# The token stage starts with the first pair of images while the second is relaid, its norm's sums come from the added rows, and tokens are normalised in place

## The reference

```
x2 = input of layer 2 (kept)        # residual of the scans
y  = scans(norm(x2)) + x2           # "rows", NCHW
n  = group_norm(y)                  # 48 channels in 16 groups, per image
t  = n.reshape(b, h*w, 48)          # the same bytes, read as tokens of 48
h  = gelu(gelu(t @ W1 + b1))        # 16 hidden, 8 + 8
u  = x1 * gate(layernorm(x2half))   # depthwise 3x3 + pointwise + product
out = y + u @ W2 + b2
```

## Time and profile before

| what | before |
|---|---|
| median of 3 runs | 2882.09 us |
| the profiled execution | 2881.06 us, span 2879.3 us |
| PE busy | 2431.3 us, 84% |
| DVE busy | 1431.1 us, 50% |
| ACT busy | 835.9 us, 29% |
| POOL busy | 250.1 us, 9% |
| end of the last scan | about 2424.4 us |
| first instruction of `affine(0)` | 2597.9 us |
| reduction of line 1324 in `mlp(0)`, (1), (2), (3) | 2636.1, 2702.3, 2764.7, 2828.9 us |

### The profile page before, as it was taken

One profiled execution on the slowest core, in us unless ns is written; L12 is line 12 of the kernel. 1 busy time (PEld: TensorE's weight loads), 2 busy tenths in 40 slices (PEclk: granted clock), 3 DMA queues, 4 the chain that ended last, 5 costly groups with the idle time before them and its releaser, 6 DMA issues.

```text
span 2879.3 us, 47164 instructions
## 1 busy us (share of the span) xinstructions
PE 2431.3 (84%) x18580; PEld 2126.0 (74%) x18580; DVE 1431.1 (50%) x3238; ACT 835.9 (29%) x1347; POOL 250.1 (9%) x244
## 2 busy tenths in 40 slices
PE   2999999999998899999999608999999996006876
PEld 2999939849832899999999608999999996002433
DVE  3323263353365444445555664444455555785565
ACT  3433353353456002430035320024300353002221
POOL 1000000000000720000000130000000001453110
PEclk9999999999999999999999859999999998557988
DMA  8840000012003200000000292000000001573333
GB/s 153 144 72 4 1 1 1 1 31 58 1 1 86 47 1 1 1 1 1 1 1 1 39 267 46 1 1 1 1 1 1 1 1 44 176 262 88 88 88 88
DMA packets 52147, 129.90 MB, mean 45 GB/s; under 512 B 9728, under 2 KB 34656, under 8 KB 45504
## 3 DMA queue, kind: packets, MB, share of 16 engines
q1 hardware_dynamic: 48864, 113.92, 16.6%
q10 hardware_dynamic: 2976, 13.34, 1.5%
q0 software_dynamic: 128, 0.01, 0.0%
HBM read 76.91 MB, written 50.33 MB: 44 GB/s over the span
## 4 chain that ended last, share of the span: by engine, by line
PE 78%; DVE 7%; DMA 6%; ACT 4%; issue 3%; POOL 1%; SPq 0%; ACTq 0%; DVEq 0%; POOLq 0%
PE bank L938 17%; PE bank L939 15%; PE bank L940 15%; PE bank L841 13%; PE bank L903 5%; PE bank L856 3%; PE bank L846 3%; ACT work L616 3%; DMA flat_rows<-work 2%; PE bank L975 2%; DVE work L319 2%; DMA work<-saved 2%; PE bank L1033 1%; DMA work<-in_x 1%; PE bank L966 1%
## 5 line engine op out<-in xcount | busy, mean ns | idle before, releaser
L1242 DVE TENSOR_TENSOR image<-bank,image 112x128 f32<-112x128 f32 x2032 | 666.7, 328 | 710.3 <-PE bank L940 710.3
L938 PE MATMUL bank<-image,scan_wt 112*112 112x128 f32 x4064 | 810.9, 280 | 36.8 <-ACT image L690 30.2
L939 PE MATMUL bank<-image,scan_wt 112*112 112x126 f32 x4064 | 770.7, 271 | 0.0
L940 PE MATMUL bank<-image,scan_wt 112*112 112x126 f32 x4064 | 769.4, 270 | 0.0
L938 PEld LDWEIGHTS bank<-image,scan_wt 112*112 112x112 f32 x4064 | 566.6, 175 | 44.2 <-ACT image L690 30.3
L939 PEld LDWEIGHTS bank<-image,scan_wt 112*112 112x112 f32 x4064 | 581.0, 176 | 0.0
L940 PEld LDWEIGHTS bank<-image,scan_wt 112*112 112x112 f32 x4064 | 578.4, 176 | 0.0
L841 PE MATMUL bank<-work 112*128 112x192 f32 x2304 | 423.4, 332 | 10.5 <-issue 10.5
L616 ACT ACTIVATE work<-image,gn_shift,gn_scale 48x567 f32<-48x567 f32 (+5 forms) x384 | 334.8, 904 | 314.3 <-PE bank L846 220.3
L708 ACT COPY work<-image 48x256 f32 (+1 forms) x256 | 109.5, 428 | 978.1 <-PE bank L940 977.6
L841 PEld LDWEIGHTS bank<-work 112*128 112x128 f32 x2304 | 374.5, 192 | 12.9 <-issue 12.4
(11 more groups left out here) (142 smaller groups left out, 1651.6 us busy)
## 6 DMA issues: line engine op xcount, KB each, us to landing
work<-saved SPq DMA_DIRECT2D x64, 384.0 KB, 8.6
flat_rows<-work ACTq DMA_DIRECT2D x32, 384.0 KB, 7.5
image<-flat_rows SPq DMA_DIRECT2D x4, 3072.0 KB, 14.5
out<-image SPq DMA_DIRECT2D x8, 1536.0 KB, 8.1
saved<-image SPq DMA_DIRECT2D x12, 768.0 KB, 10.0
saved<-image SPq DMA_DIRECT2D x6, 1536.0 KB, 16.4
band<-in_x SPq DMA_DIRECT2D x16, 384.0 KB, 5.7
work<-in_x SPq DMA_DIRECT2D x16, 384.0 KB, 5.6
```

The costliest lines, as they stand in the source:

```text
L938: mm(dst, wt[:, 1], src, start=True, stop=False)
L939: mm(dst[:, 1:J2, :], wt[:, 0], src[:, 0:J2 - 1, :], start=False, stop=False)
L940: mm(dst[:, 0:J2 - 1, :], wt[:, 2], src[:, 1:J2, :], start=False, stop=True).then_inc(s_prod[g], 1)
L1242: v.tensor_tensor(line(g, along_w, at), prod, line(g, along_w, src), ALU.add).then_inc(s_state[g], 1)
```

## The change

- The fourth scan of the last layer goes without `exchange`: the result stays split by row parity, and the relayout takes it from there.
- The relayout adds on DVE alone, two instructions of 112 x 1024 for a block (`relayout(t)`, 16 blocks). The sum goes into a part of `image` that is free by then (the first block into `nat`), so no block waits for an earlier one to be sent. `x2` comes into five buffers `kept`; the first five blocks are brought during the last scans.
- A block is sent in four DMAs of 192 KB with runs of 512 bytes in `flat` (`send_rows`): for the first pair the `LO` half by SP and the `HI` half by ACT, for the second pair all four by SP.
- The statistics come from the added rows in SBUF (`rows_stats`, four `bn_stats` of 112 x 512 for a block), not from the loaded tokens, and the group norm runs for each pair; a matrix `group_tok` spreads the sums to the token layout.
- Tokens of images 0 and 1 are loaded when the first pair is sent, and `affine` works in place in `toks`. DVE relays the first pair, takes its statistics, relays two blocks of the second pair, does `affine(0)`, then the other six blocks, three blocks' statistics, `affine(1)`, and the last five blocks' statistics inside `mlp(0)`. Images 2 and 3 get their norm behind `mlp(0)`.
- `residual(b)` waits until PE has turned all tokens of image b (before: until `affine(b)`), as it overwrites them. POOL adds b2 in eight instructions of 768 columns.
- ACT alone takes the turned tokens of image 0, and waits for the last relayout before its gelu. POOL builds its constants for the MLP during the last scans.

```diff
+        def send_rows(queue, t, parity):
+            g, n = t // NBLK, t % NBLK
+            for i in range(2):
+                queue.dma_start(lines[parity, 2 * g + i, :, n * BLK:(n + 1) * BLK, :],
+                                rows_home(t)[(LO, HI)[parity], i, :].rearrange("p (k w) -> p k w", k=BLK))\
+                    .then_inc(s_flat[g][i] if n else s_first[g], 16)
...
+            def bring_kept(t):
+                g, n = t // NBLK, t % NBLK
+                for parity, rows in enumerate((LO, HI)):
+                    sp.dma_start(kept[t % KEPT][rows, :].rearrange("p (w n) -> p w n", w=2),
+                                 halves[:, :, g, parity, n * 2 * BN:(n + 1) * 2 * BN]).then_inc(s_x2[t % KEPT], 16)
+
+            def bring_tokens(b):
+                sp.wait_ge(s_stat, X_STATS + 2 * NB + 1 + b // 2)
+                sp.wait_ge(s_first[b // 2], 64)
+                sp.wait_ge(s_flat[b // 2][b % 2], 32 * (NBLK - 1))
                 sp.dma_start(toks[:, b, :], flat[b].rearrange("(p n) -> p n", p=128)).then_inc(s_tok[b], 16)
+
+            for t in range(KEPT):
+                bring_kept(t)
+            for t in range(NBLK):
+                sp.wait_ge(s_res, t + 1)
+                send_rows(sp, t, 0)
+                if t + KEPT < NBLK:
+                    bring_kept(t + KEPT)
+            for t in range(NBLK, NBLK + KEPT):
+                bring_kept(t)
+                if t == NBLK + 2:
+                    bring_tokens(0)
+            for t in range(NBLK, 2 * NBLK):
+                sp.wait_ge(s_res, t + 1)
+                send_rows(sp, t, 0)
+                send_rows(sp, t, 1)
+                if t + KEPT < 2 * NBLK:
+                    bring_kept(t + KEPT)
+                if t == NBLK:
+                    bring_tokens(1)
+            bring_tokens(2)
+            bring_tokens(3)
...
             def residual(b):
-                sp.wait_ge(s_xn, b + 1)
+                sp.wait_ge(s_xt_p, (b + 1) * GROUPS)
...
+                    for c in range(0, C, SLICE):
+                        last = nc.gpsimd.tensor_tensor(v[:, c:c + SLICE, :], ...
+                    last.then_inc(s_b2, 1)
...
+                if layer == 1:
+                    break
...
+            act.wait_ge(s_res, 2 * NBLK)
             gelu_twice(0)
+            act.wait_ge(s_first[1], 64)
+            act.wait_ge(s_xn, 2)
+            mlp(0, True)
...
+            mlp(0, True)
+            pe.wait_ge(s_add, 2 * NQ + TWO)
+            token_sums(7, 2, NB)
...
+            def relayout(t):
+                g, n = t // NBLK, t % NBLK
+                dve.wait_ge(s_x2[t % KEPT], 32 * (t // KEPT + 1))
+                if t:
+                    dve.wait_ge(s_res, t)
...
+                for i in range(2):
+                    last = v.tensor_tensor(o[:, i], state[:, i], x2[:, i], ALU.add)
+                last.then_inc(s_res, 1)
...
+            relayout(NBLK)
+            relayout(NBLK + 1)
+            dve.wait_ge(s_tok[0], 16)
             affine(0)
+            for t in range(NBLK + 2, 2 * NBLK):
+                relayout(t)
+            for t in range(3):
+                rows_stats(NBLK + t)
+            dve.wait_ge(s_tok[1], 16)
+            affine(1)
...
+            mlp(0, True, False, rows_stats)
+            dve.wait_ge(s_stat, X_STATS + 2 * NB + 2)
+            group_norm(7, P, NSTAT, 2, NB)
+            for b in range(2, NB):
+                dve.wait_ge(s_tok[b], 16)
+            affine(2)
```

More of the change, by code:

```diff
@@ L181, in build @@
         at += 16 * C
[L182 to L190 removed]
+        assert at <= WORK - IN_COLS, at
+        nat = cut(0, [CHUNK], P)
+        at = WORK - KEPT * CHUNK
+        kept = [cut(at + i * CHUNK, [CHUNK], P) for i in range(KEPT)]
+        back = kept[0:PER]
+        swap_tmp = cut(at - 256, [2, 64, 2], P)
+        toks = image[:, :].rearrange("p (b n) -> p b n", b=NB)[:, :, 0:TCOLS]
+        hid = image[:, TCOLS:IMG]
         x_t = [cut(i * 512, [512]) for i in range(2)]
[L192 removed]
+        n_pad = cut(1024, [G, GW])
+        at = 1024 + G * GW
         w1_sb = cut(at, [2 * HID], 97)
@@ L206, in build @@
         at += 5 * 128
-        assert at <= 13300, at
+        assert at <= WORK, at
         gdw_sb = gates[:, 0:72]
@@ L490, in _ @@
                 pool.wait_ge(s_state[g], 1)
-            for m in range(PER):
-                nc.gpsimd.memset(back[m][32:HALF, :], 0.0).then_inc(s_back_gap, 1)
-            pool.wait_ge(s_back_gap, PER)
+            for m in range(KEPT):
+                nc.gpsimd.memset(kept[m][32:HALF, :], 0.0).then_inc(s_back_gap, 1)
+            pool.wait_ge(s_back_gap, KEPT)
             pool.wait_ge(s_const, 16 * N_CONST)
@@ L1039, in _ @@
             pe.wait_ge(s_band, N_BAND + G + 1)
-            with pe.Fori(0, NB - 1) as b:
-                mlp(b, True)
-            mlp(NB - 1, False)
+            mlp(0, True)
+            pe.wait_ge(s_add, 2 * NQ + TWO)
+            token_sums(7, 2, NB)
+            for b in range(1, NB):
+                mlp(b, b + 1 < NB)
         @block.vector
@@ new lines, in rows_stats @@
+            def rows_stats(t):
+                g, n = t // NBLK, t % NBLK
+                dve.wait_ge(s_res, t + 1)
+                for i in range(2):
+                    for h in range(2):
+                        last = take_stats(P, 2 * g + i, 2 * n + h, rows_home(t)[:, i, h * BN:(h + 1) * BN])
+                if n == NBLK - 1:
+                    last.then_inc(s_stat, 1)
+            for t in range(NBLK):
+                relayout(t)
+            for t in range(NBLK):
+                rows_stats(t)
@@ L1340, in row_norm, with mlp @@
                                     ALU.add).then_inc(s_ln, 1)
-            def mlp(b, more, even_more):
+            def mlp(b, more, even_more, behind=None):
                 for i in range(4):
                     row_norm(b, i)
+                    if behind and i < 2:
+                        behind(NBLK + 3 + i)
                     if more:
@@ L1349, in mlp @@
                     take_tokens(b + 1, g)
+                for t in range(5, NBLK if behind else 0):
+                    behind(NBLK + t)
                 dve.wait_ge(s_gt_p, 8 * b + 6)
@@ L1381, in mlp @@
                                         ALU.add).then_inc(s_add, 1)
+            relayout(NBLK)
+            relayout(NBLK + 1)
+            dve.wait_ge(s_tok[0], 16)
             affine(0)
+            for t in range(NBLK + 2, 2 * NBLK):
+                relayout(t)
+            for t in range(3):
+                rows_stats(NBLK + t)
+            dve.wait_ge(s_tok[1], 16)
+            affine(1)
+            dve.wait_ge(s_xn, 2)
             dve.wait_ge(s_gate_zero, 2)
             dve.wait_ge(s_gate_w, 16 * N_GATE)
-            for g in range(1, GROUPS, 2):
-                take_tokens(0, g)
-            affine(1)
-            with dve.Fori(0, NB - 2) as b:
-                chain.enter(b, MLP_LINKS)
-                mlp(b, True, True)
-                chain.leave(NB - 2)
-            mlp(NB - 2, True, False)
-            mlp(NB - 1, False, False)
+            dve.wait_ge(s_first[1], 64)
+            mlp(0, True, False, rows_stats)
[4 more added lines that the diff above has]
+            affine(2)
+            for b in range(1, NB):
+                mlp(b, b + 1 < NB, b + 2 < NB)
 def kernel(**inputs):
```

180 lines of the change are left out of this document (77 added, 103 removed).

## The result

The changed kernel takes 2784.28 us (median of four runs, 2780.75 to 2788.44) against 2879.49 us for the kernel before beside it: a ratio of 0.9677, with a 95% interval of 0.9645 to 0.9709. The forecast was 2780. The execution that was profiled is the slowest of the four, 2788.44 us with a span of 2786.6.

What follows compares the result with a forecast made beforehand. The end stage was taken as latency behind latency, no engine or queue near its limit. -3.8 - 119.0 + 7.3 + 24.9 - 7.8 - 5.3 + 2.5 = -101.2 from 2881.06 gives 2780 us, own range 2764 to 2794.

Steps and rivals of the forecast that it cites:

- Scans (a): Fourth scan of the last layer, without the exchange beside it: 3.8 us less, bounds 0 to 5.
- To `affine(0)` (b): From the last scan step to the start of `affine(0)`: 54.5 us instead of 173.5, a gain of 119.0.
- To the first reduction (c): From `affine(0)` to the reduction of `mlp(0)`: 45.5 us instead of 38.2, a loss of 7.3.
- To the second reduction (d): Reduction of `mlp(0)` to that of `mlp(1)`: 91.0 us instead of 66.15, a loss of 24.9, with image 0's residual late.
- The rest: Later stretches, through holds by POOL's add: `mlp(1)` gains 7.8 us, `mlp(2)` gains 5.3, `mlp(3)` loses 2.5.
- One transfer at a time: Rival: stores and loads of blocks do not overlap in SP's queue; 2805 us, chance 0.20.
- The residual is not late: Rival: image 0's residual comes early enough, so reduction to reduction takes 66 us; 2755 us in all, chance 0.08.
- The 512-byte sends: Rival: slow sends make the kernel slower than before; at 50 GB/s 121 us more, 2901 us, chance 0.03.
- DVE's relayout was held: Rival: the relayout is held at every block, 5 us for each of eight, 40 in all; 2820 us, chance 0.07.

Runs made afterwards that it cites:

- e9: The changed kernel with all sends of the first pair held until its eight blocks are added: 2788.95 us.
- e2: The changed kernel with the load of a block ahead of the sends in SP's queue, and the tokens of image 1 later: 2772.52 us.
- e1: The changed kernel with the residual of image 0 issued ahead of the tokens of images 2 and 3: 2763.84 us.
- e5: The changed kernel with POOL adding b2 in one piece instead of eight: 2783.00 us.
- e4: The changed kernel with sends in runs of 4 KB instead of 512 bytes, so the output is not the reference's: 2777.62 us.
- e7: The changed kernel with e1 and e2 together, plus the second pair's upper halves sent from GpSimd's queue: 2755.72 us.

## Why the prediction was right, step by step

**Scans (a): right.** 3.8 us were forecast, 3.9 measured (685.5 less 681.6). The rate is that of the earlier trace rows without the exchange. The changed kernel, the stretch that had 230 adds before, columns as the earlier trace rows:

```profile
2260.00:2420.00 160.00, 160.00 (x1408) 159.57 (x1408) 82.92 (x235) 0.00 (x0) 0.00 (x0) 1.00 0.00 1
```

In the profiled execution it does not show in the time, since the layer began 3.9 us later there.

**To `affine(0)` (b): the order of events right, 4 us too short.** The step that failed is "They run beside the loads: stores and loads together moved 389 GB/s". First, the row was misread. A load of a layer's kept input, ahead of layer 2, has 8 KB from each partition (384 KB over 48), a save there 32 KB (1536 KB over 48). The packets of the kernel before in the second and in the third stretch of the earlier trace rows:

```profile
DMA packets 166, 1.01 MB, mean 168 GB/s; under 512 B 43, under 2 KB 43, under 8 KB 43
```

```profile
DMA packets 100, 2.33 MB, mean 389 GB/s; under 512 B 28, under 2 KB 28, under 8 KB 28
```

Without the small ones that is 123 packets of 8 KB, which are loads, and 72 of 32 KB in the mean, which are saves. So 168 is what loads move alone, as 179 is, and 389 is what two saves from the two halves move with next to no load beside them. No row of before shows stores and loads together, or sends of blocks alone. The changed kernel in the stretch where both are under way:

```profile
2432.00:2452.00 20.00, 0.00 (x0) 0.00 (x0) 11.46 (x10) 0.00 (x0) 0.00 (x0) 0.50 1.09 301
```

Both together got 301 GB/s, with the DMA engines full. A block of each is 1.57 MB and so 5.2 us, and the last two of the three blocks came 6.6 and 5.9 us after the one before, not 4.4. The eighth add ended at 27.7 instead of 22.5, and at 20.0 in e9. Of the 7.8 us between these two, some 4 to 6 are the sends in flight and some 2 to 4 the loads' place behind the sends in SP's queue (the kernels with loads first). The 4.7 us for a block's sends, taken from the 168, were too long as well: 243 GB/s (e9) make it 3.2. It did no harm, as the statistics, and not the end of the sends, opened the way for the tokens. The statistics (19.00 us for 32) and the norm (4.3) were as forecast. The load of the tokens started the moment the statistics ended; it was issued at 46.8 instead of 44 and took 11.71 us instead of 10.44, and so 5.2 us of lateness at the adds became 4.0 at `affine(0)`.

**To the first reduction (c): 4.6 us too short.** The step that failed is that SP's issues cost 5.3 us "beneath the 9 us in which the block's load and send pass". SP's issues in the changed kernel:

```profile
2486.57 1.01 SPq L447 DMA_DIRECT2D image<-flat_rows  x1
2487.62 16.01 SPq L334 DMA_DIRECT2D flat_rows<-image  x4
2503.67 3.33 SPq L440 DMA_DIRECT2D work<-saved  x2
2507.05 3.64 SPq L334 DMA_DIRECT2D flat_rows<-image  x4
2510.73 1.97 SPq L440 DMA_DIRECT2D work<-saved  x2
```

Four issues took 16.01 us behind the tokens of image 1, and the load of the next block could not be issued before. The last `x2` was added at 96.6, where 87.7 was forecast. With the loads ahead of the sends and the tokens of image 1 later (e2) the last add ended at 77.95 and the stretch took 38.25. So the order in SP's queue cost all of (c): 7.3 us forecast, 11.9 measured, none with the other order.

**To the second reduction (d): right, 89.28 for 91.0.** The wait was 27.65 us where 20 to 28 were forecast, and e1 shows that it was the queue's order: with the residual first the stretch took 69.96. The clock fell meanwhile, as rows ahead of the wait's end show (the column behind POOL; 0.81 over the whole stretch, 0.90 before): 0.77 in the mean while PE ran out of work, then 0.50, the lower level, with PE idle.

```profile
2572.00:2588.00 16.00, 4.13 (x16) 1.68 (x14) 0.44 (x1) 7.61 (x9) 0.00 (x0) 0.77 1.02 325
2588.00:2600.00 12.00, 0.00 (x0) 0.00 (x0) 0.00 (x0) 0.00 (x0) 11.39 (x8) 0.50 0.88 243
```

**The rest: the sum right, its reason in part not.** 54.6, 58.9 and 52.9 were forecast and 52.36, 57.21 and 54.70 measured, 2.1 us less in all. The sum gave the gain of `mlp(2)`, 5.3 us, to the eight parts. With one part (e5) the stretch is 5.7 us shorter than before, through the earlier start of POOL's add; with eight it is 7.0 shorter in the changed kernel and 10.2 in e9, at a granted clock of 0.91 and 1.00. So both may have a part, the clock has one of some 3 us, and that 57.21 came near 58.9 is luck of this execution. `mlp(3)` lost 4.3 us where 2.5 were forecast: its three held instructions took 3.4 us over their own. `mlp(1)` gained 2.2 us more than the hold of POOL's add; the granted clock there is 0.97, and was 0.92, which goes with it, but no run separates the two.

**The rivals.** "One transfer at a time" has something in it. The transfers do not overlap as the forecast took them, and each is late by what stands ahead of it. But its 2805 went too far: loads and sends together moved 301 GB/s, where loads alone moved 179 and 168 and the sends alone 243 (e9). The page named in the forecast for it (the Trainium skill, "SBUF — State Buffer", section "Can I just issue two DMAs to hit both halves?") has two transfers on the two halves serialize because all share the same engines. Here the share of the engines, 0.97 to 1.09, agrees that they are the resource, but the 301 GB/s are more than either kind moved alone. The 389, which the forecast set against that rule for opposite directions, says nothing of them. "The residual is not late" was what a change of order makes true (e1); the forecast's 25 us for it were 19.3. The 512-byte sends were not the danger: they moved 243 GB/s alone (e9), and longer runs (e4) bring 6.7 us in the medians, within the scatter. The 300 GB/s that the forecast set against this danger was no sign: its 1023 packets for 2.10 MB in the earlier trace rows hold 2 KB each, those of the sends 512 bytes. And DVE's relayout was held, but at three blocks and for 8.4 us, not at eight for 40.

In sum, counted in the profiled execution: 4.0 + 4.6 - 1.7 - 2.1 are 4.8 us more than forecast behind the last scan step, and 3.9 us from the later start of the layer make 8.7; 2779.9 + 8.7 is 2788.6, against 2788.44 measured. That the median lies only 4.3 us from the forecast is in part luck: misses of both signs cancel, and the layer's start alone scatters by more than that.

## What to carry to other kernels

When latency is taken out of a stage, price what remains by bytes: take the share of the DMA engines in the stage after the change, and all transfers in one sum, rather than a best rate from one row; and see by the packets' size which transfers such a row holds before it is read as two kinds at once. In a queue that issues in order, put first what somebody waits for next (here the load of the next block, and the residual of the image at work); two changes of such order brought another 31 us without touching an instruction of the compute engines. And ask of each wait that is forecast whether a line moved in the queue's program would make it go away.

## What the runs showed of the hardware that was not expected

- The issue of a DMA can take as long as the transfers ahead of it: four sends took 16.01 us to issue behind a 3 MB load that landed 20.0 us after its own issue, where an issue took 0.88 us before. All that stands behind in the same program is held too. Sending half of the blocks from another engine's queue (e7) did not shorten the whole measurably.
- Sends in 512-byte runs moved 243 GB/s alone (e9), loads of a kept input 179 alone, both together 301. Cutting the packets to a third (22797 to 6673) raised the rate of the relayout from 257 to 280 GB/s only.
- A DVE instruction of two columns takes 0.16 us alone and up to 1.39 beside POOL's adds; one of 1.2 us was held 5.88 by a single POOL add. Cut into eight, POOL's add held three instructions by 0.1 to 1.3 us each.
- The same stretch with the same code took 57.21 us at a granted clock of 0.91 and 54.03 at 1.00 (the changed kernel and e9, `mlp(2)`).
